# Four-bit stage: the overlapped last half chunk of the down product done with three passes over zeroed weight rows, and one VectorE subtraction of 768 columns in place of two

## The reference, cut to what matters

```python
def fp4_linear(x, w):
    xq = fp4_quant_dequant(x)      # blocks of 16, grid 0 .. 6, scale = max/6
    wq = fp4_quant_dequant(w)
    return jnp.einsum('bsk,nk->bsn', xq, wq)
gate = fp4_linear(x, w_gate)       # 256 -> 704
y = fp4_linear(x, w_up)            # 256 -> 704
h = jax.nn.silu(gate) * y
return fp4_linear(h, w_down)       # 704 -> 256
```

## Time and profile before

| | |
|---|---|
| median of three runs | 2656.07 us |
| the three runs | 2645.53, 2656.07, 2657.33 us |
| span of the profiled execution | 2660.2 us |
| mean granted TensorE clock | 0.944 |
| TensorE, VectorE, ScalarE, POOL busy | 90%, 67%, 49%, 27% of the span |
| the four-bit stage's turns | from about 450 to 995 us of the span |

### The profile page before, as it was taken

The page is one execution under the profiler, slowest core; times in us unless marked ns, Lnnn a source line. Parts: engine busy times, 40 slices in busy tenths (PEclk is TensorE's granted clock), DMA queues, the critical chain, the costliest instruction groups (busy, mean ns, idle before and its releaser), DMA issues. The chain is left out here.

```text
span 2660.2 us, 43690 instructions
## 1 busy us (share of the span) xinstructions
PE 2396.7 (90%) x15960; PEld 2204.5 (83%) x15960; DVE 1794.1 (67%) x3357; ACT 1297.3 (49%) x2026; POOL 710.9 (27%) x468
## 2 busy tenths in 40 slices
PE   6988896798999978999999999993999999499999
PEld 6887885788888877988988898883899999399998
DVE  5566665899999966566566566544667765777774
ACT  4344443334433324464454455444566665356555
POOL 1011011444444433123123023113244441211111
PEclk9999997899999998999999999975999999699999
DMA  5000000000000000000000000002000010000000
GB/s 171 0 0 0 0 0 18 2 1 0 0 0 0 1 1 17 13 8 12 16 4 12 16 6 9 16 9 64 17 24 24 16 48 1 34 19 30 24 24 32
DMA packets 42971, 45.69 MB, mean 17 GB/s; under 512 B 3088, under 2 KB 41872, under 8 KB 42640
## 3 DMA queue, kind: packets, MB, share of 16 engines
q1 hardware_dynamic: 42896, 44.69, 5.1%
HBM read 27.90 MB, written 16.78 MB: 17 GB/s over the span
## 5 line engine op out<-in xcount | busy, mean ns | idle before, releaser
L1842 DVE TENSOR_TENSOR m_a_lo<-m_a,m_a_hi 128x512 fp32r<-128x512 f32 x128 | 107.3, 839 | 126.4 <-ACT m_a_hi L1800 126.4
L1796 ACT ACTIVATE d_a<-d_ps_wide,d_b,d_w_gain 128x512 f32<-128x512 f32 x128 | 100.1, 782 | 136.7 <-PE d_ps_wide L271 134.4
L1269 POOL TENSOR_TENSOR p_kf<-p_kf,p_k_shift 128x1024 f32<-128x1024 f32 x64 | 119.4, 1904 | 155.4 <-DVE p_k_shift L1403 155.4
L1755 PE MATMUL m_ps_z<-m_w_hi,m_a_hi 128*128 128x256 f32 x512 | 147.4, 288 | 9.2 <-DVE m_w_lo L1821 9.2
L1796 ACT ACTIVATE m_a<-m_ps_wide,m_b 128x512 f32<-128x512 f32 x128 | 88.0, 688 | 121.3 <-PE m_ps_wide L271 121.2
L1755 PE MATMUL m_ps_z<-m_w_hi,m_a_lo 128*128 128x256 f32 x512 | 145.6, 284 | 0.0
L1755 PE MATMUL m_ps_z<-m_w_lo,m_a_hi 128*128 128x256 f32 x512 | 145.3, 284 | 0.0
L1755 PE MATMUL d_ps_z<-d_w_hi,d_a_hi 128*128 128x256 f32 x512 | 143.6, 280 | 1.1 <-DVE d_a_lo L1842 1.1
L1755 PE MATMUL d_ps_z<-d_w_lo,d_a_hi 128*128 128x256 f32 x512 | 143.4, 280 | 0.0
L1755 PE MATMUL d_ps_z<-d_w_hi,d_a_lo 128*128 128x256 f32 x512 | 142.6, 278 | 0.0
L1842 DVE TENSOR_TENSOR d_a_lo<-d_a,d_a_hi 128x512 fp32r<-128x512 f32 x128 | 85.8, 689 | 77.1 <-ACT d_a_hi L1800 72.5
(11 more groups left out here) (361 smaller groups left out, 8580.1 us busy)
## 6 DMA issues: line engine op xcount, KB each, us to landing
residual<-in_x SPq DMA_DIRECT2D x8, 1024.0 KB, 11.8
attn<-p_attn SPq DMA_DIRECT2D x32, 256.0 KB, 2.1
m_attn<-attn SPq DMA_DIRECT2D x16, 512.0 KB, 3.7
out<-residual SPq DMA_DIRECT2D x16, 512.0 KB, 2.9
raw_weights<-in_d_q SPq DMA_DIRECT2D x2, 1024.0 KB, 7.1
d_scale<-in_d_scale SPq DMA_DIRECT2D x2, 1024.0 KB, 5.3
raw_weights<-in_m_w1T SPq DMA_DIRECT2D x1, 1024.0 KB, 5.1
raw_weights<-in_m_w2T SPq DMA_DIRECT2D x1, 1024.0 KB, 7.5
```

Of the source, the lines that this page charges most:

```text
L1269: pool.tensor_tensor(f, f, k_shift[:, i, :].unsqueeze(2).broadcast_to([P, HEADS, M]), ALU.subtract).then_inc(k_shifted, 1)
L1755: mm = pe.matmul(z, a, w[:, f, :], start=(f == 0 and k == 0 and j % 2 == 0), stop=(f == FC - 1 and k == 2), skip_group_check=True)
L1796: act.activation(self.a[f % RING][:, :], self.ps_wide[f % 2][:, :], self.func, bias=self.b1[:, f:f + 1], scale=gain(f))
L1842: dve.tensor_tensor(self.a2[1][:, f, :], self.a[f % RING][:, :], self.a2[0][:, f, :].bitcast(F32), ALU.subtract).then_inc(self.a_lo, 1)
```

## The change

The last half chunk is treated as every other chunk. The weights of its first 64 rows are zero in both parts, hi and lo, so the repeated rows of h add nothing whatever they hold. `split_h` is one subtraction over all 768 columns, `narrow` is six ordinary products, 18 passes where there were 17, and the semaphore `h_lo` counts one per tile where it counted two. In the preparation of the weights one copy of 64 x 256 out of PSUM becomes a memset of the same size.

```diff
--- before.py
+++ after.py
@@ -820,7 +820,7 @@
 
                 dve.wait_ge(w_lo, len(fills))
                 dve.memset(down_w[1][0:FL, KF - 1, :].bitcast(F32), 0.0).then_inc(w_lo, 1)
-                dve.tensor_copy(down_w[0][0:FL, KF - 1, :], ps_w[(len(fills) - 1) % 4][FL:P, 0:D]).then_inc(w_lo, 1)
+                dve.memset(down_w[0][0:FL, KF - 1, :].bitcast(F32), 0.0).then_inc(w_lo, 1)
                 dve.wait_ge(w_lo, len(fills) + 2)
 
             @block.tensor
@@ -956,11 +956,7 @@
                 def phase(t, s):
                     dve.wait_ge(h_hi, G * t + j + 1)
                     hi, lo = h_T[j]
-                    full = (KF - 1) * P
-                    dve.tensor_tensor(lo[:, 0:full], ps_h[:, 0:full], hi[:, 0:full].bitcast(F32), ALU.subtract).then_inc(h_lo, 1)
-
-                    dve.tensor_tensor(hi[0:FL, full:KF * P], ps_h[FL:P, full:KF * P], hi[FL:P, full:KF * P].bitcast(F32),
-                                      ALU.subtract).then_inc(h_lo, 1)
+                    dve.tensor_tensor(lo[:, :], ps_h[:, 0:KF * P], hi[:, :].bitcast(F32), ALU.subtract).then_inc(h_lo, 1)
                 return phase
 
             pipeline(dve, N, [(8, add_down), (4, split_n), (7, split_h(0)), (3, round_n), (6, round_h), (5, multiply(0)),
@@ -1041,7 +1037,7 @@
             def turn_h(j):
                 def phase(t, s):
                     pe.wait_ge(h_quantised, t + 1)
-                    wait_count(pe, h_lo, 2 * (G * t + j))
+                    wait_count(pe, h_lo, G * t + j)
                     for c in range(KF):
                         at = j * FF + min(c * P, FF - P)
                         mm = pe.transpose(ps_h[:, c * P:(c + 1) * P], h_q[s][:, at:at + P], ident[:, :])
@@ -1052,15 +1048,11 @@
                 def phase(t, s):
                     if j == 0:
                         wait_count(pe, x_updated, t)
-                    pe.wait_ge(h_lo, 2 * (G * t + j + 1))
+                    pe.wait_ge(h_lo, G * t + j + 1)
                     out = ps_down[:, j * D:(j + 1) * D]
-                    for c in range(KF - 1):
-                        product(pe, out, part(h_T[j], slice(None), slice(c * P, (c + 1) * P)), part(down_w, slice(None), c),
-                                start=(c == 0), stop=False)
-
-                    last = h_T[j][0][:, (KF - 1) * P:KF * P]
-                    pe.matmul(out, last, down_w[0][:, KF - 1, :], start=False, stop=False)
-                    mm = pe.matmul(out, last, down_w[1][:, KF - 1, :], start=False, stop=True)
+                    for c in range(KF):
+                        mm = product(pe, out, part(h_T[j], slice(None), slice(c * P, (c + 1) * P)), part(down_w, slice(None), c),
+                                     start=(c == 0), stop=(c == KF - 1))
                     mm.then_inc(down_done, 1)
                 return phase
```

## The result

The changed kernel takes 2608.67 us, the median of five runs (2607.55 to 2622.40); the kernel before, run beside it, 2656.07 (2645.53 to 2662.07). The ratio is 0.9842, with a 95% interval of 0.9812 to 0.9872: 1.6% faster, 42 us by the ratio and 47 by the medians. The forecast was 2645.2 us with a range of 2637 to 2655, and 0.71 on no change above 0.5%. It had the direction and missed the size: a gain of 10.9 us was forecast, four times as much came.

The account below looks back on a forecast made before the run. VectorE's loop through POOL and ScalarE was taken to bound the turn: 13.3 us over 27 turns, less 0.35, gives 13.0; two clock falls at 1.07 each leave 10.9, from 2656.07 to 2645.2 us, range 2637 to 2655.

Parts of the forecast that it names:

- The loop: Four-bit stage: VectorE's `round_h` to `scales_h` (11.47 us), then POOL and ScalarE (4.18 us), end each 15.65 us turn.
- The saving of `split_h(0)`: VectorE, tile 0: its time stands beside POOL and ScalarE, so what it saves only makes VectorE wait for ScalarE.
- The longer subtraction: VectorE's `split_h` over 768 columns: 948 ns, next instruction 0.87 us after its start, saving 0.30 us a tile.
- no overlap: Rival, chance 0.15: the new subtraction holds VectorE for 0.98 us, so 3.0 us less gain; 2648 us.
- What `split_h(1)` saves shortens the loop: VectorE, tile 1: the 0.30 us saved comes off every full-clock turn, 15.65 to 15.35 us.
- The clock term: TensorE idles less, so of eight turns with falls to low clock two stay; each gives back 1.07 us.
- The slack on the up passes: TensorE's up passes end 1.0 us before `multiply(1)` needs them; about 0.6 after, still covered at full clock.
- the slower rival: Chance 0.06: TensorE's path to the up passes ends turns at low clock; 15.9 us slower in all 27, 2672 us.
- The rest of the program: Outside the four-bit stage: the change touches one stage only; the preparation's memset for a copy, nothing either way.

Follow-up runs that it names:

- before_port: The kernel before, with the 32 maxima per partition of n kept in PSUM instead of SBUF and nothing of the change: 2606.4 us, ratio 0.9841.
- filler_spare: The changed kernel with an extra subtraction of 288 columns into an unread spare tile ahead of `split_h(1)`: 2633.7 us, ratio 0.9943.
- before_again: The kernel before, unchanged, run once more for a second profile: 2637.1 us.
- after_again: The changed kernel, unchanged, run once more for a second profile: 2601.0 us.
- split_two: The changed kernel with `split_h` as two subtractions, 640 and 128 columns, both over all 128 partitions: 2603.9 us, ratio 0.9825.
- before_shift: The kernel before, with four multiplications by 1.0, some 2 us of delay, ahead of the linear-attention stage: 2656.6 us, ratio 1.0031.

## Why the prediction was wrong

- **The loop** (`round_h` to `scales_h` on VectorE, then POOL and ScalarE) was right. The saving of `split_h(0)` was lost beside POOL and ScalarE, and in part inside a row: L189 on n, a mean of 0.73 us in the kernel before, now starts 0.3 to 0.4 us before POOL has divided h in two of three turns and takes a mean of 0.93 (28 of each).
- **The longer subtraction** was right: 0.95 and 0.86, against 0.948 and 0.87; "no overlap" fell.
- **The step that failed** is the sum of the VectorE part of the loop. "What `split_h(1)` saves shortens the loop" took every other instruction of that part as fixed, and the prediction said that VectorE had no wait on another engine between 742.10 and 753.57. It had one, for POOL, inside L172. Worked from the rows, the part from `round_h` on is shorter by 0.31 for the pair, by 0.58 for L172 (748.12 to 749.04 before, 751.25 to 751.59 after) and by 0.12 for L191 to L927; `multiply(1)` then waits 0.21 longer (0.55 for the up passes against 0.34 for its scales). 0.31 + 0.58 + 0.12 - 0.21 = 0.80 a turn, 21.6 us in 27 turns, against the 8.1 of the forecast (27 x 0.30). before_port comes to the same 14.85 with the pair as it was: L172 to L173 is 0.11 us there instead of 0.92, and that alone makes the turn 0.8 shorter (`multiply(1)` then waits 0.33, as it did for its scales before). In the changed kernel L172 starts 0.45 us earlier after L191 on h than before (3.91 against 4.36) and so 0.35 us ahead of POOL's restore of n instead of 0.10 behind it; this is what the pair's 0.31 and the 0.12 did above all. The row that would have told it was in the timeline: the instruction behind the earlier trace rows's L170, 1.01 us for 32 columns, five times the same form on 88 columns a moment later.
- **The clock term** was right: one fall left in the steady turns, the first of them (16.48 us), where I took two. With 5.2 us of excess before and 1.9 after it gives 3.3, and 21.6 + 3.3 = 24.9. before_port, with the old TensorE work in the shorter turn, and filler_spare, with the new work in the old turn, also have one fall left, so here either half of "more work, shorter turn" was enough.
- **The slack on the up passes** of 0.6 us came out as a wait of 0.55, 0.21 beyond the 0.34 for the scales: TensorE's path ends the turn, because VectorE is there 1.0 us earlier and not 0.30. The mechanism of the slower rival exists; it came with a shorter turn, not with a low clock.
- **The rest of the program** was taken as unchanged, and the range as the scatter of three runs. The two profiles differ by 15.2 us in the linear-attention stage. 4 slow blocks more at 2.46 and one half slow are about 11 of them; the other 4 lie in its seven earlier batches. In before_again and after_again a batch in which the clock never falls takes 94.1 or 94.8 us, and one with a fall 96.6 to 98.5. before_again to after_again is 36.2 of span with no slow block in either; 22.9 of it is the four-bit stage and 11 are these batches, whose table of stretches shows the same work, for before_again and then after_again:

```profile
1081.00:1759.80 678.80, 664.01 (x4620) 601.84 (x4619) 409.57 (x698) 351.85 (x482) 151.86 (x111) 0.97 0.03 11
...
1055.80:1723.50 667.70, 654.38 (x4621) 594.24 (x4619) 405.88 (x698) 351.89 (x482) 151.91 (x111) 0.99 0.03 11
```

678.8 us at a granted clock of 0.97 against 667.7 at 0.99. The step of the prediction that failed here is the term that it put at nothing: the four-bit stage gives 23 to 24 us, and by the profiles the rest of the 42 to 47 lies in the linear-attention stage, at its clock. It is not the luck of one set of runs, since before_port (0.9841) and split_two (0.9825) have it too. Why a start some 20 us earlier should go with the high clock, and 2 us of delay undo it, is not settled by these runs.

## What to carry to other kernels

Before an edit on VectorE is priced, compare each instruction of the loop with others of its own form: one whose duration doesn't fit its columns may be waiting inside its row, and moving it by a third of a microsecond can be worth more than the edit. Ask of GpSimd's neighbours which of its instructions each VectorE `tensor_scalar` falls beside, and put one operand in PSUM where it matters. Here an operand that starts at partition 64 cost the neighbours too, down to the next reader of PSUM. And a stage whose TensorE waits in every short block can run at either clock, so that a change ahead of it can move the whole by more than its own worth: compare two profiles stage by stage, and take each twice, before a difference is put down to the edit.

## What the runs showed of the hardware that I had not expected

- A VectorE `tensor_scalar` of 32 columns takes 0.18 to 1.29 us, by what is left of POOL's instruction of the moment (that rest, less 0.14 us, on top of its own time); 0.19 in 32 of 32 turns with a PSUM source, though POOL was at work.
- A read of PSUM from partition 64 still costs 0.12 us at the next read of PSUM from partition 0, with four instructions between them.
- The falls of the clock in the four-bit stage come in the same eight steady turns, with the same lengths within 0.02 us, in two profiles of the kernel before (before and before_again). In before_shift, whose code is the same up to there, there are eight again, but two of them come two turns later. The slow blocks of the later stage are six in the first, none in the second and six in the third.
- 2 us of delay ahead of that stage made the changed kernel 24 us slower by the medians (2632.5 against 2608.7, in different sets of runs; by the ratios to the kernel before, 0.9939 against 0.9842, 26 us).
